# A Sinkhorn attention in groups of three heads instead of four, two groups to a bank of rows, one started every five cycles

## What is computed

```python
qn = q / norm(q)
C = where(eye, 1000, 1 - qn @ qn.T)          # 512 x 512
log_K = -C / 0.1
log_v = 0
for _ in range(10):
    log_u = log_marg - logsumexp(log_K + log_v[None, :], axis=-1)
    log_v = log_marg - logsumexp(log_K + log_u[:, None], axis=-2)
z = exp(log_u[:, None] + log_K + log_v[None, :])
z = where(eye, 1, z / max(z))
out = softmax(z * 0.25) @ v
```

## Time and profile before

| | us |
|---|---|
| median of 3 runs | 5091.24 |
| lowest and highest run | 5083.55, 5093.23 |
| the profiled execution | 5082.8 |
| its span | 5081.0 |
| PE busy in the span | 4568.4 |
| DVE busy | 3744.7 |
| ACT busy | 3051.0 |
| POOL busy | 310.8 |

### The profile page before, as it was taken

The page is one execution under the profiler, slowest core; times in us unless marked ns, Lnnn a source line. Parts: engine busy times, 40 slices in busy tenths (PEclk is TensorE's granted clock), DMA queues, the critical chain, the costliest instruction groups (busy, mean ns, idle before and its releaser), DMA issues. The chain is left out here.

```text
span 5081.0 us, 191812 instructions
## 1 busy us (share of the span) xinstructions
PE 4568.4 (90%) x84561; PEld 3640.2 (72%) x84562; DVE 3744.7 (74%) x8549; ACT 3051.0 (60%) x4474; POOL 310.8 (6%) x349
## 2 busy tenths in 40 slices
PE   5999999885999999999999999999999278599990
PEld 4777777642788888888888888888888144377770
DVE  8999999743577777777777777777777644355557
ACT  4777777633566666666666666666664234377771
POOL 0000000000000000000000000000000014433330
PEclk9999999986999999999999999999999576699995
DMA  1000000032000000000000000000000222322214
GB/s 63 33 35 27 27 27 27 29 98 66 14 16 17 22 16 16 22 17 16 16 23 16 16 21 17 16 16 23 16 12 9 92 89 97 112 69 67 71 60 152
DMA packets 164003, 203.02 MB, mean 40 GB/s; under 512 B 66736, under 2 KB 141744, under 8 KB 160752
## 3 DMA queue, kind: packets, MB, share of 16 engines
q1 hardware_dynamic: 149680, 159.86, 10.5%
q0 software_dynamic: 13632, 32.66, 1.8%
HBM read 123.64 MB, written 68.81 MB: 38 GB/s over the span
## 5 line engine op out<-in xcount | busy, mean ns | idle before, releaser
L653 PE MATMUL y_ps<-k_sb,x_sb 128*12 128x256 f16 x58368 | 1683.4, 273 | 13.3 <-DVE x_sb L890 13.0
L653 PEld LDWEIGHTS y_ps<-k_sb,x_sb 128*12 128x12 bf16 x58368 | 1425.6, 88 | 186.9 <-issue 24.4
L772 ACT ACTIVATE y_sb<-y_ps 128x256 f32<-128x256 f32 x912 | 348.3, 382 | 841.8 <-PE y_ps L653 841.8
L781 ACT ACTIVATE k_new<-cos,k_bias 128x512 f32<-128x512 f32 x768 | 520.9, 683 | 171.2 <-PE cos L680 171.2
L663 PEld LDWEIGHTS turned_x<-rows_in,y_sb 128*128 128x128 f32 x3648 | 477.7, 191 | 118.3 <-issue 71.6
L921 DVE CUSTOM_DVE_ANT_0 plan<-plan,u_rows,v_last 128x512 f32<-128x512 f32 x768 | 535.2, 744 | 4.3 <-issue 0.3
L663 PE MATMUL turned_x<-rows_in,y_sb 128*128 128x16 f32 x3648 | 526.6, 258 | 8.4 <-ACT y_sb L772 8.2
L256 PE MATMUL acc<-w_hl,feat_h 128*128 128x384 f16 x2688 | 454.6, 327 | 87.5 <-ACT feat_h L241 87.5
L795 ACT ACTIVATE plan<-plan,p_bias,p_scale 128x1024 f32<-128x1024 f32 x384 | 464.2, 1238 | 9.7 <-DVE p_scale L932 9.7
L909 DVE TENSOR_TENSOR plan<-k_sb 128x1024 f32<-128x1024 f16 x384 | 459.3, 1217 | 0.0
L936 DVE TENSOR_TENSOR k_sb<-k_new,k_sb 128x2048 f16<-128x2048 f32 x192 | 436.1, 2272 | 30.4 <-ACT k_sb L789 30.4
(11 more groups left out here) (256 smaller groups left out, 7199.3 us busy)
## 6 DMA issues: line engine op xcount, KB each, us to landing
x_in_sb<-expert_rows SPq DMA_DIRECT2D x39, 528.0 KB, 3.7
xt<-in_x_dram SPq DMA_DIRECT2D x16, 1280.0 KB, 5.9
q_left<-q_parts SPq DMA_DIRECT2D x192, 64.0 KB, 3.0
q_right<-q_parts SPq DMA_DIRECT2D x192, 64.0 KB, 3.0
y<-expert_results SPq DMA_DIRECT2D x32, 384.0 KB, 3.7
v_parts<-v_sb SPq DMA_DIRECT2D x16, 408.0 KB, 2.4
v_in_sb<-v_parts SPq DMA_DIRECT2D x48, 136.0 KB, 3.5
h_tokens<-h_sb SPq DMA_DIRECT2D x16, 384.0 KB, 2.5
```

The lines of the kernel that those rows point to most:

```text
L653: last = nc.tensor.matmul(y[a][32 * c:32 * c + XW, :, :], high[:, j, XW * h:XW * (h + 1)], k_sb[s][:, h, :, at:at + P], start=(h == 0 and ...
L772: nc.scalar.activation(y_sb[a][:, :, :], y[a][:, :, :], ACT.Copy).then_inc(rows_read[a], 1)
L781: nc.scalar.activation(k_new[h % 2][:, c, :], cos[:, c % 2, :], ACT.Exp, bias=k_bias[:, 0:1], scale=1.0 / (REG * Q_SCALE ** 2), accum_out= ...
```

## The change

`attend` is reordered; the matmuls and elementwise operations of a head stay, as do the other three blocks.

- Groups have `GROUP = 3` heads, 64 groups. Group g starts in cycle `5 g` and takes 19 cycles, so that up to four are in flight. Even groups use bank 0 and odd ones bank 1 for all their 19 steps; the two groups of a bank are read, turned and split together. The stationary side has 18 columns (two groups x three heads x three parts) instead of 12, the turn's moving side 24 instead of 16, and the split works on 24 elements a partition. x of the two groups stands in slots of one `x_sb`, with a step of 64 between chunks and 21 between heads.
- `k_sb` is a ring of 16 heads. The q tiles have two buffers instead of three.
- Each head has its own rhythm: a cycle has three points, a head begins every five points, and each piece of the building and finishing has a fixed offset (`BUILD`, `FIN`). So the pieces fall into the cycles in a pattern that comes back after five cycles (three heads).
- On PE a cycle is: multiply of bank 0, point, multiply of bank 1, turn_x, turn of bank 0, point, turn of bank 1, point. On VectorE: point, next_x(0), point, next_x(1), point. Inside a point VectorE does join, scale_of, times_u, normalise, low_parts and `start(g)` (the split of the row sums) in this order; `start(g)` falls into the last point of cycle `5 g - 1`.
- The set-up on GpSimd has nine instructions instead of three.

```diff
-GH = 4
-GROUPS_PER_IMAGE = HEADS // GH
-ALL_GROUPS = IMAGES * GROUPS_PER_IMAGE
+GROUP = 3
+ALL_HEADS = IMAGES * HEADS
+ALL_GROUPS = ALL_HEADS // GROUP
+PER_IMAGE = HEADS // GROUP
 REG, ITERS = 0.1, 10
-YOUNG, OLD = 9, 10
-CYCLES = 10
-XW = 3 * GH
-XS = XW + 3
+STEPS, APART = 2 * ITERS - 1, 5
+LAST_CYCLE = APART * (ALL_GROUPS - 1) + STEPS - 1
+BUILD, FIN = -23, 55
+FIRST_POINT, LAST_POINT = BUILD, 5 * (ALL_HEADS - 1) + FIN + 12
+K_RING = 16
+XROW, XW, XS = 64, 6 * GROUP, 7 * GROUP
+XSLOT = TB * XROW + 3 * GROUP
+COLS = 2 * TB * GROUP
...
+def head_at(point, offset):
+
+    H, rest = divmod(point - offset, 5)
+    return H if rest == 0 and 0 <= H < ALL_HEADS else None
+
+
+def active(m, cycle):
+
+    return [(g, cycle - APART * g) for g in range(max(m, cycle // APART - 4), min(cycle // APART, ALL_GROUPS - 1) + 1)
+            if g % 2 == m and 0 <= cycle - APART * g < STEPS]
...
-            def multiply(a, G, s, i):
-
-                if a == 0 and i == 0:
-                    after(pe, first_x, G + 1)
-                elif a == 0:
-                    after(pe, x_new[0], G * YOUNG + i)
-                elif i == 0:
-                    after(pe, x_new[0], G * YOUNG)
-                else:
-                    after(pe, x_new[1], (G - 1) * OLD + i)
-                high = x_sb[s][:, :, :].bitcast(BF16).rearrange("p b (w two) -> p b w two", two=2)[:, :, :, 1]
-                for h in range(GH):
+            def multiply(m, cycle):
+
+                groups = active(m, cycle)
+                if not groups:
+                    return
+                after(pe, x_new[m], step_of(m, cycle))
+                heads = sorted(((g // 2 % 2, h, g) for g, age in groups for h in range(GROUP)))
+                for g, age in groups:
+                    if age == 0:
+                        after(pe, first_x, g + 1)
+                        after(pe, k_built, (g + 1) * GROUP)
+                for e, h, g in heads:
                     for j in range(TB):
+                        window = e * TB * XROW + j * XROW + h * XW
                         for c in range(TB):
                             at = j * TOKENS + c * P
-                            last = nc.tensor.matmul(y[a][32 * c:32 * c + XW, :, :], high[:, j, XW * h:XW * (h + 1)],
-                                                    k_sb[s][:, h, :, at:at + P],
-                                                    start=(h == 0 and j == 0), stop=(h == GH - 1 and j == TB - 1))
-                last.then_inc(product[a], 1)
-
-            def turn(a, n):
-
-                after(pe, rows_read[a], n + 1)
-                after(pe, x_new[a], n)
+                            last = nc.tensor.matmul(y[m][32 * c:32 * c + XW, :, :], halves[m][:, window:window + XW],
+                                                    k_sb[:, (g * GROUP + h) % K_RING, :, at:at + P],
+                                                    start=((e, h, g) == heads[0] and j == 0),
+                                                    stop=((e, h, g) == heads[-1] and j == TB - 1))
+                last.then_inc(product[m], 1)
+
+            def turn(m, cycle):
+
+                if not active(m, cycle):
+                    return
+                n = step_of(m, cycle)
+                after(pe, rows_read[m], n + 1)
+                after(pe, x_new[m], n)
                 for part in range(2):
-                    last = nc.tensor.matmul(tr_flat[a], y_sb[a][:, part, :], add_parts, start=(part == 0), stop=(part == 1))
-                last.then_inc(turned[a], 1)
-
-            def turn_x(G, s, build):
-                if build:
-                    after(pe, k_exp, (G + 2) * (GH * TB) - 1)
-                high = x_sb[s][:, :, :].bitcast(BF16).rearrange("p (c b) (w two) -> p c (b w) two", c=2, two=2)[:, :, :, 1]
-                for c in range(2):
-                    last = nc.tensor.matmul(xt_ps[:, c, :], high[:, c, :], eye_bf[:, :], start=True, stop=True)
-                last.then_inc(x_turned, 1)
-
-            def cosines(G, s, h, half):
-                H = (G + 1) * GH + h
-                after(pe, k_exp, H * TB + 2 * half)
-                for c in (2 * half, 2 * half + 1):
-                    nc.tensor.matmul(cos[:, c % 2, :], q_left[s][:, h, c * P:(c + 1) * P], q_right[s][:, h, :],
-                                     start=True, stop=False)
-                    last = nc.tensor.matmul(cos[:, c % 2, c * P:(c + 1) * P], eye_h[:, :], eye_hide[:, :], start=False, stop=True)
-                last.then_inc(cos_ready, 1)
-
-            def u_to_rows(F, h):
-                after(pe, xt_ready, F + 1)
-                after(pe, scale_ready, F * GH + h)
+                    last = nc.tensor.matmul(tr_flat[m], y_sb[m][:, part, :], add_parts, start=(part == 0), stop=(part == 1))
+                last.then_inc(turned[m], 1)
+
...
+            def u_to_rows(H):
+                g, h = H // GROUP, H % GROUP
+                after(pe, xt_ready, g + 1)
+                after(pe, scale_ready, H)
                 for c in range(TB):
-                    last = nc.tensor.matmul(u_rows[:, c * P:(c + 1) * P], pick[:, c % 2 * GH + h, :], xt_sb[:, c // 2, :],
+                    last = nc.tensor.matmul(u_rows[:, c * P:(c + 1) * P], pick[:, c % 2, g // 2 % 2, h, :], xt_sb[:, c // 2, :],
                                             start=True, stop=True)
...
+            def point(q):
+                for c in range(TB):
+                    H = head_at(q, BUILD + c)
+                    if H is not None:
+                        cosines(H, c)
+                H = head_at(q, FIN + 5)
+                if H is not None:
+                    max_to_rows(H)
+                H = head_at(q, FIN + 1)
+                if H is not None:
+                    u_to_rows(H)
+                H = head_at(q, FIN + 9)
+                if H is not None:
+                    times_v(H)
+                H = head_at(q, FIN + 11)
+                if H is not None:
+                    turn_v(H)
+
+            for cycle in range(FIRST_CYCLE, END_CYCLE):
+                multiply(0, cycle)
+                point(3 * cycle)
+                multiply(1, cycle)
+                for m in range(2):
+                    turn_x(m, cycle)
+                turn(0, cycle)
+                point(3 * cycle + 1)
+                turn(1, cycle)
+                point(3 * cycle + 2)
...
+            def next_x(m, cycle):
+                groups = active(m, cycle)
+                if not groups:
+                    return
+                going = sorted(g // 2 % 2 for g, age in groups if age < STEPS - 1)
+                after(dve, turned[m], step_of(m, cycle) + 1)
+                for g, age in groups:
+                    if age == STEPS - 1:
+                        done = nc.vector.reciprocal(v_last[g % 2][:, :, :], tr[m][:, g // 2 % 2])
+                        if not going:
+                            done.then_inc(x_new[m], 1)
+                if going:
+                    slots = slice(going[0], going[-1] + 1)
+                    split(tr[m][:, slots], m, slots, x_steps[m], steps_before(m, cycle), x_new[m])
+
+            def start(g):
+                e = g // 2 % 2
+                after(dve, k_exp, (g + 1) * GROUP * TB)
+                after(dve, x_turned, g - 3)
+                split(row_sums[g % 2][:, :, :].unsqueeze(1), g % 2, slice(e, e + 1), first_steps, 2 * g, first_x)
...
+            def scale_of(H):
+                after(dve, max_rows_ready, H + 1)
                 nc.vector.tensor_reduce(all_max[:, :], max_rows, AX_X, ALU.max).then_inc(all_max_ready, 1)
...
+            def point(q):
+                for half in range(2):
+                    H = head_at(q, FIN + half)
+                    if H is not None:
+                        join(H, half)
+                H = head_at(q, FIN + 5)
+                if H is not None:
+                    scale_of(H)
+                for half in range(2):
+                    H = head_at(q, FIN + 2 + half)
+                    if H is not None:
+                        times_u(H, (2 * half, 2 * half + 1))
+                H = head_at(q, FIN + 12)
+                if H is not None:
+                    normalise(H)
+                H = head_at(q, BUILD + 7)
+                if H is not None:
+                    low_parts(H)
+                if (q + 1) % (3 * APART) == 0 and 0 <= (q + 1) // (3 * APART) < ALL_GROUPS:
+                    start((q + 1) // (3 * APART))
+
+            for cycle in range(FIRST_CYCLE, END_CYCLE):
+                point(3 * cycle)
+                next_x(0, cycle)
+                point(3 * cycle + 1)
+                next_x(1, cycle)
+                point(3 * cycle + 2)
```

More of the change, by code:

```diff
@@ L570, in attend, with step_of, steps_before @@
         block = ctx.enter_context(nc.Block())
[L571 to L591, removed]
+        SELECTS = 9
+        CONSTS, ZEROS = 7, SELECTS + 4
+        FIRST_CYCLE, END_CYCLE = FIRST_POINT // 3, LAST_POINT // 3 + 1
+        def step_of(m, cycle):
```

(37 more changed lines are left out.)

422 lines of the change are left out of this document (148 added, 274 removed).

## The result

| | before | after |
|---|---|---|
| median of the runs, us | 5089.02 (4 runs) | 5368.62 (4 runs) |
| lowest and highest | 5083.55, 5093.23 | 5357.36, 5381.35 |
| the profiled execution | 5082.8 | 5381.35 |
| its span | 5081.0 | 5379.4 |
| ratio of the times, 95% interval | | 1.0551 (1.0521 to 1.058) |

The change makes the kernel 5.5% slower, 280 us by the medians, 298 us between the two profiled executions. The prediction was 5305 us, slower, with a range to 5400.

The account below looks back on a forecast made before the run. The prediction took TensorE's instruction stream as the bound. From 5082.8 us it added 190 for 180 steady heads (waits less saved work), took off 10 for the ends, added 41 for the clock: 5304, forecast 5305, range 5190 to 5400.

Parts of the forecast that it names:

- The bound: In the attention stage before, TensorE's instruction stream sets the time: 13.92 us a head.
- The work: On TensorE, ten cycles (six heads) take 80.6 us without waits; 18 columns add nothing, at most 58 us.
- a, first_x: Multiply starts at S+6.51 (S: bank 0's turn starts behind bank 1's run); TensorE waits 4.2 us even, 0.85 odd groups.
- b, u_to_rows: On TensorE, u_to_rows waits for VectorE's scale_of: 1.55 us twice and 0.5 us twice in ten cycles.
- The sum of the waits: TensorE's waits for first_x and ahead of u_to_rows together: 9.2 us in ten cycles.
- rival 2: No wait to speak of: TensorE's other work covers the vector chain; 4981 us, faster; chance 0.10.
- c, the clock: TensorE falls to 1.2 GHz behind 4.2 us waits: 24 falls of 1.7 us, 41 us; ends 0 and 90.
- rival 3: Shorter u_to_rows waits also bring the clock down, or loaded ScalarE adds to each: 109 us more, 5410; chance 0.10.
- rival 4: The wider stationary side of the y_ps matmuls is exposed on TensorE: +58 us, 5360; chance 0.05.
- Rival 1: Waits for first_x and at u_to_rows as forecast, clock at 1.00 throughout: 5263 us; chance 0.20.

Follow-up runs that it names:

- a3: The changed kernel with u_to_rows one point later on TensorE and start(g) two points earlier on VectorE; 5013.88 us, ratio 0.9805 to before.
- a6: The changed kernel with u_to_rows one point later and 62 unread matmuls filling TensorE's wait for first_x of even groups; 5160.2 us, ratio 1.0085.
- a9: The changed kernel, order unmoved, with unread matmuls filling waits: 62 ahead of first_x of even groups, 26 ahead of u_to_rows of each group's first head; 5282.44 us.
- a1: The changed kernel with start(g) two points earlier on VectorE, in the first point of cycle 5g - 1; 5269.68 us, ratio 1.0296.
- a5: The changed kernel with 62 unread matmuls filling TensorE's wait for first_x of even groups, order unmoved; 5360.11 us, ratio 1.0491.
- a7: The changed kernel with u_to_rows one point later and start(g) ahead of low_parts in the same point; 5075.34 us, ratio 0.9919.

## Why the prediction was right, and where it was not

**The bound.** TensorE's list in order, with nothing idle in before, was the right reading: in a3 it is full again, and the time follows its work.

**The work.** Predicted 80.6 us a round without waits, 2.9 less than before: 86 us over the 180 heads of the steady part, and 10 at the ends. The terms of that sum add up to 80.8, not 80.6. a3 has 81.44, which is 2.05 less than before, and a stage 85 us shorter instead of 96. The price of 18 columns was taken at nothing with 58 us as its upper end: the 26.6 ns between matmuls bear that out. The Trainium skill's "TensorE: Matmul & The Clock Gate", section "LDWEIGHTS (loading the stationary operand)", has a formula by which a load grows with its columns; the trace shows that no such growth reached the path: the 290 us of a fully exposed load did not appear.

The 0.6 us a round that a3 lies above 80.8 are one dearer piece less several cheaper ones. From start to start in the round of a3, the 24 chunks of cosines take 8.25 us, 0.34 each, of which some 0.4 in all are waits of `times_v` for its weights. The prediction had 0.27 each, 6.5 us, read where two chunks stand together; before has 0.28 for its 16 in a phase. The new order puts each chunk by itself. The other pieces came out 1.2 us cheaper, `u_to_rows` alone by 0.6 (0.23 each for 0.32). No run keeps the chunks in pairs, so what that would give back is not shown.

**a, first_x.** Predicted start at S + 6.51, measured S + 6.44; predicted wait 4.2 us for an even group, measured 3.86, since TensorE was free at S + 2.58 and not at S + 2.31. The piece 2.95 from `low_parts` to the first multiply, taken whole from the earlier trace rows, is 2.96 here (2303.28 to 2306.24). The split of 24 columns is 0.70 (2302.58 to 2303.28), predicted 0.69; the one before it has only 12 columns and takes 0.58, which is the whole difference to S + 6.51. For odd groups the chain on VectorE was right too (S + 6.45), but the wait was 0.26, not 0.85: TensorE, foreseen at S + 5.66, came at S + 6.19, by the dearer single cosines and a wait of `times_v` for its weights. Both kinds together were predicted at 5.05 us a round, 4.12 in the round looked at, 4.2 by a6 against a3.

**b, u_to_rows.** Predicted 1.55 twice and 0.5 twice a round; read in one round: 1.64 and 1.69, 0.40 and 0.38. 123.3 us in all are 4.0 for each of some 31 rounds, against 4.1.

**The sum of the waits** was 9.2 us a round. The round looked at has 1.64 + 1.69 + 0.40 + 0.38 + 3.86 + 0.26 = 8.2, and some 0.4 more where `times_v` waits for weights, which a3 has too; a9 against a3 gives 8.31. Over the stage it is 264 us, predicted 276 (9.2 x 30). So rival 2, in which TensorE's other work covers the vector chain, is out, by 8.3 us a round; the row of 13 us for all of before was true of an order that kept a cycle between maker and user.

**c, the clock, is the term that was mis-sized.** Predicted 24 falls of 1.7 us, 41 us, with 0 and 90 as ends; measured 85, near the upper end. Two things were off. A fall behind the long pause lasted 6.8 us, the whole multiply with it, and not the 3.45 us of the earlier trace rows, and cost 2.4 us instead of 1.7: after has 25 of these, one each 92.2 us, from 1843 us on, and two before; the 25 make 60 of the 85 us. And there were ten short ones before that, between 1376 and 1741 us. Three of them stand behind the long pause, seven behind a pause of `u_to_rows` of 1.56 to 1.61 us, no longer than those that cost nothing later on. The row of one, with 48 matmuls in 2.74 us where 2295.28 above has 1.49:

```profile
1644.73 0.38 PE L700 MATMUL u_rows<-xt_sb,pick 128*128 128x128 bf16 x4 [1.56 <-DVE p_scale L917]
...
1645.49 2.74 PE L658 MATMUL y_ps<-k_sb,x_sb 128*18 128x256 f16 x48
```

A few more come where the stage empties. So part of rival 3 ("the shorter waits of b bring the clock down too"), given 0.10, was at work in after itself, in its first rounds; a1 and a5 show it throughout the stage, with 63 and 49 falls, where the long pause is gone or filled. The Trainium skill's page "TensorE: Matmul & The Clock Gate", section "HAM oscillation", tells of a loop whose idle gaps of 3 to 5 us put the engine back to half rate each time, for some 1.67 us a gap, of which half is lost. The steady part of after agrees in kind, with one pause of 3.7 us and one fall a round, and not in size: the multiply runs 5.0 us at 0.52, and 2.4 us are lost. The falls of a1 behind pauses of 1.60 us, at 1.5 us each, and their absence in nearly every round of a7 at 1.49, that section doesn't foresee.

Expected 5305 for a profiled execution of before of 5083: +221 us in the stage by the sum, measured +264. The 43 us between them are 44 of clock and 11 of smaller saving, less 12 for the waits. The rest of the profiled 5381 is the 34 us behind the stage, for which the prediction had no term; the median, 5368.62, is 13 below the profiled execution. The number alone would not have told the mechanisms apart: rival 4's 5360 lies nearer to 5368.62 than the forecast, and rival 3's 5410 is nearer too. What speaks for the forecast's path is the waits, read to within 0.1 us at first_x on VectorE, and a3 and a9.

**Rival 1**, waits with the clock held, is what a9 is: 5263 was 1.035 times the 5083 of before, and a9 measured 1.0324.

## What to carry to other kernels

When one list of instructions is full and a change regroups the work, price the order as well as the work: for each hand-over, add up what stands ahead of it on the maker's list and on the user's from a common point, with start-to-start distances. Here that sum was right to a tenth of a microsecond on VectorE's side and to half of one on TensorE's, and it also named the cure: two steps moved by one and two points took 264 us of waits and 85 us of clock off, and left the saving of 85. A pause on TensorE can cost more than its length (2.4 us more in after, nothing in nearly every round of a7), and in these runs that was not a property of the pause alone: take all pauses of a loop away or fill them all, and judge by the time of the loop, not by whether the clock held behind the one that was treated.

## What the hardware showed that I had not expected

- The same pause brings the clock down in one kernel and not in the next, and in one kernel at one time and not at another. 1.56 to 1.61 us ahead of `u_to_rows`: down every half round in a1, about three times in two rounds in a5, seven times in the first rounds of after, never in its steady part. 1.49 us once a round in a7: two falls from 1400 us on.
- The falls keep step with the loop: 92.2 us apart in after (its round 92.15), 44.37 apart in a1 (half its round of 88.75). Which of several pauses gets the fall isn't told by its length alone. What decides between them stays open.
- Filling one of the pauses left the total nearly as it was (3024 and 3014 us); filling both took 85 us off, though the waits stayed.
- Stationary tiles of 18 columns for 12, on four strips of rows, with 256 moving columns: 26.6 ns from matmul to matmul, for 26.8.
